# Ordering the key blocks of windowed attention by parity, in a macaron transformer kernel on one core

## What is computed

```python
w = WINDOW                                   # 32 tokens; 16 heads of 64 columns
bq, bk, bv = (t.reshape(b, h, nw, w, d) for t in (q, k, v))

def look(t):                                 # each window also sees the one before it
    p = jnp.pad(t, ((0, 0), (0, 0), (1, 0), (0, 0), (0, 0)))
    return jnp.concatenate([p[:, :, :nw], p[:, :, 1:]], axis=3)
bk2, bv2 = (look(bk), look(bv))              # 64 keys for 32 queries
mask = (it < jb) | (it > jb + w) | (jb == -1)
sim = jnp.einsum('bhwie,bhwje->bhwij', bq, bk2) * QK_SCALE
attn = jax.nn.softmax(jnp.where(mask, -jnp.finfo(sim.dtype).max, sim), -1)
out = jnp.einsum('bhwij,bhwje->bhwie', attn, bv2)
```

## Time and profile before

| | |
|---|---|
| Three runs, median | 3705.6 us |
| Lowest and highest | 3697.82 and 3710.14 us |
| Span of the profiled execution | 3698.0 us |
| Mean granted TensorE clock in it | 0.963 |
| TensorE matmul (PE) busy | 3345.2 us, 90% |
| TensorE weight load (PEld) busy | 2152.2 us, 58% |
| VectorE busy | 2824.4 us, 76% |
| GpSimd busy | 2338.6 us, 63% |
| ScalarE busy | 2242.4 us, 61% |
| DMA queue 1, share of 16 engines | 29.4%, 280.54 MB |

### The profile page before, as it was taken

The page is one execution under the profiler, slowest core; times in us unless marked ns, Lnnn a source line. Parts: engine busy times, 40 slices in busy tenths (PEclk is TensorE's granted clock), DMA queues, the critical chain, the costliest instruction groups (busy, mean ns, idle before and its releaser), DMA issues. The chain is left out here.

```text
span 3698.0 us, 147404 instructions
## 1 busy us (share of the span) xinstructions
PE 3345.2 (90%) x61692; PEld 2152.2 (58%) x61692; DVE 2824.4 (76%) x4178; ACT 2242.4 (61%) x4098; POOL 2338.6 (63%) x2167
## 2 busy tenths in 40 slices
PE   5899999999989999986998889999999999999997
PEld 2666666666666666663222566666666666666664
DVE  4888888888887888873232877878888888888883
ACT  3566766666665666652664555656666666566663
POOL 4777777776676787761000767667677767667762
PEclk8999999999999999997999999999999999999998
DMA  4334334333333333321000223333333323323321
GB/s 121 80 79 126 85 88 115 80 101 100 80 97 96 84 104 81 85 62 33 1 1 6 74 72 82 82 78 94 82 80 95 91 67 103 74 68 102 82 65 38
DMA packets 216860, 289.97 MB, mean 78 GB/s; under 512 B 61068, under 2 KB 105864, under 8 KB 215304
## 3 DMA queue, kind: packets, MB, share of 16 engines
q1 hardware_dynamic: 216200, 280.54, 29.4%
HBM read 43.43 MB, written 10.49 MB: 15 GB/s over the span
## 5 line engine op out<-in xcount | busy, mean ns | idle before, releaser
L1165 POOL TENSOR_TENSOR rot<-t 128x512 f32<-128x512 f32 x768 | 974.4, 1272 | 310.8 <-DVE t L1024 303.4
L1171 POOL TENSOR_TENSOR qkn<-rot,rn 128x512 f32<-128x512 f32 x768 | 792.1, 1042 | 180.8 <-DVE rn L1047 180.8
L1023 DVE TENSOR_TENSOR t<-ps,table 128x512 f32<-128x512 f32 x768 | 525.8, 685 | 155.2 <-ACT sq L853 148.7
L1177 POOL TENSOR_TENSOR prob<-prob,rsum 128x512 f32<-128x512 f32 x192 | 296.7, 1545 | 394.4 <-DVE rsum L1066 393.7
L1024 DVE TENSOR_TENSOR t<-ps,table 128x512 f32<-128x512 f32 x768 | 521.7, 679 | 0.0
L692 PE MATMUL sv_all<-pT,arena 64*64 64x32 f32 x24576 | 418.9, 221 | 85.4 <-issue 85.4
L624 PE MATMUL ps<-w_pair,in_hi 128*128 128x512 f16 x1152 | 450.1, 391 | 34.7 <-POOL in_lo L1192 15.7
L853 ACT ACTIVATE sq<-ps 128x512 f32<-128x512 f32 x768 | 443.3, 600 | 38.6 <-PE ps L626 36.8
L859 ACT ACTIVATE arena<-ps 128x512 f32<-128x512 f32 x384 | 226.5, 590 | 393.4 <-PE ps L626 390.2
L1030 DVE TENSOR_REDUCE n<-sq 128x16 f32<-128x1024 f32 x384 | 464.0, 1208 | 0.0
L692 PEld LDWEIGHTS sv_all<-pT,arena 64*64 64x64 f32 x24576 | 391.3, 136 | 124.5 <-issue 124.4
(11 more groups left out here) (125 smaller groups left out, 5100.3 us busy)
## 6 DMA issues: line engine op xcount, KB each, us to landing
arena<-arena SPq DMA_DIRECT2D x1152, 128.0 KB, 2.4
arena<-arena SPq DMA_DIRECT2D x768, 64.0 KB, 2.0
w_pair<-w_split SPq DMA_DIRECT2D x44, 256.0 KB, 4.6
w_stage<-in_L_ffn_Wqkv SPq DMA_DIRECT2D x6, 1536.0 KB, 8.5
w_split<-split SPq DMA_DIRECT2D x30, 256.0 KB, 2.5
wo_sb<-in_L_ffn_Wo SPq DMA_DIRECT2D x12, 512.0 KB, 4.3
xsh<-xs SPq DMA_DIRECT2D x48, 128.0 KB, 2.5
f_in<-xs SPq DMA_DIRECT2D x48, 128.0 KB, 2.2
```

The costliest lines, as they stand in the source:

```text
L1023: dve.tensor_tensor(t1[:, b, :].rearrange("p (h d) -> p h d", d=DH), src, cos, ALU.mult)
L1165: pool.tensor_tensor(rot[:, c, :], t1[:, c % 2, :], t2[:, c % 2, :], ALU.add).then_inc(pool_add, 1)
L1171: pool.tensor_tensor(qkn[:, 0, c, :].rearrange("p (h d) -> p h d", d=DH), rot[:, c, :].rearrange("p (h d) -> p h d", d=DH), rn[:, c, :].un ...
```

## The change

The 32-token blocks of the keys are ordered by parity: even blocks stand on partitions 0 to 31 and 64 to 95, odd ones on 32 to 63 and 96 to 127. For windows 1 and 3 the 64 keys are then two blocks of one 64-token group in their order; for windows 0 and 2 they are the two blocks in turned order, so `scores` reads the keys of even windows with the two blocks swapped (a view with a negative step), and the mask is swapped to match.

`values` makes one group g of 64 tokens at a time instead of one half of the heads. Its output for the lower heads goes to partitions 0 to 63 and that for the upper heads to partitions 64 to 127 of the same PSUM tile. So each of the three passes is two matmuls of 128 rows by 64 columns that stream 512 columns, where it was one of 128 by 128. `store_v` writes the group whole into `vt`. Windows 1 and 3 read `vt` directly; SyncE copies rows into `veven` for windows 0 and 2 alone, in four DMAs a tile: two of 32 partitions by 1024 elements each for even and odd blocks, of which the odd ones have 512 elements in tile s = 0, where no block comes before.

```diff
-V_DMAS = 2 * (WPT + 1)
+V_DMAS = 4
...
-                    for par in range(2):
-                        r = par * KEYS
-                        sp.dma_start(vw[r:r + WIN, p, 0, :], vtok[P - WIN:P, (s - 1) % TILES, par, :]).then_inc(v_loaded[s], 16)
-                        sp.dma_start(vw[r + WIN:r + KEYS, p, 0, :], vtok[0:WIN, s, par, :]).then_inc(v_loaded[s], 16)
-                        for w in range(1, WPT):
-                            sp.dma_start(vw[r:r + KEYS, p, w, :],
-                                         vtok[WIN * (w - 1):WIN * (w + 1), s, par, :]).then_inc(v_loaded[s], 16)
+                    for half_of in range(2):
+                        even = slice(half_of * KEYS, half_of * KEYS + WIN)
+                        odd = slice(half_of * KEYS + WIN, half_of * KEYS + KEYS)
+                        sp.dma_start(veven[even, p, :, :], vt[even, 2 * s:2 * s + 2, :]).then_inc(v_loaded[s], 16)
+                        if s:
+                            sp.dma_start(veven[odd, p, :, :], vt[odd, 2 * s - 1:2 * s + 1, :]).then_inc(v_loaded[s], 16)
+                        else:
+                            sp.dma_start(veven[odd, p, 1, :], vt[odd, 0, :]).then_inc(v_loaded[s], 16)
...
-                def values(T, q, s, half_of):
-
-                    pe.wait_ge(dve_rot, tile_done(T, 2 + half_of, 4))
-                    three_pass(proj[half_of][:, :], q, slice(s * P, (s + 1) * P),
-                               lambda w: w[:, 2 * INNER:].rearrange("p (j a r) -> p j a r", a=2, r=P)[:, :, half_of, :]).then_inc(pe_v, 1)
+                def values(T, q, s, g):
+
+                    pe.wait_ge(dve_rot, tile_done(T, 2 + g, 4))
+                    cols = slice(s * P + g * KEYS, s * P + (g + 1) * KEYS)
+                    for i, (x, w) in enumerate(((in_hi, w_hi), (in_hi, w_lo), (in_lo, w_hi))):
+                        for half_of in range(2):
+                            last = pe.matmul(proj[g][half_of * KEYS:(half_of + 1) * KEYS, :], x[:, q, cols],
+                                             w[:, 2 * INNER:].rearrange("p (j a r) -> p j a r", a=2, r=P)[:, :, half_of, :],
+                                             start=i == 0, stop=i == 2, skip_group_check=True)
+                    last.then_inc(pe_v, 1)
...
+                                keys = kT[r, p, pair, w * WIN:w * WIN + KEYS]
+                                if w % 2 == 0:
+                                    keys = keys.rearrange("d (b k) -> d b k", b=2)[:, ::-1, :]
...
+                                keys = vt[r, 2 * s + w // 2, :] if w % 2 else veven[r, v, w // 2, :]
...
-                    act.activation(vtok[:, s, par, :], proj[par][:, :], ACT.Copy, scale=1.0 / W_SCALE).then_inc(act_v, 1)
+                    act.activation(vt[:, 2 * s + g, :], proj[g][:, :], ACT.Copy, scale=1.0 / W_SCALE).then_inc(act_v, 1)
...
-    first[:WIN, :WIN] = MASKED
+    first[:WIN, WIN:] = MASKED
```

More of the change, by code:

```diff
@@ L133, in build @@
         kT = sb("kT", [P, 2, PAIRS, WIN + P])
-        arena = sb("arena", [P, 4 * WPT * CH])
-        vw = arena[:, 0:2 * WPT * CH].rearrange("p (a w c) -> p a w c", a=2, w=WPT)
-        vtok = arena[:, 2 * WPT * CH:].rearrange("p (s a c) -> p s a c", s=TILES, a=2)
+        arena = sb("arena", [P, 7 * P * 8])
+        vt = arena[:, 0:2 * TILES * CH].rearrange("p (s c) -> p s c", s=2 * TILES)
+        veven = arena[:, 2 * TILES * CH:(2 * TILES + 4) * CH].rearrange("p (a w c) -> p a w c", a=2, w=2)
         smax = sb("smax", [P, HEADS])
@@ L664, in scores @@
                                 r = slice(par * DH, (par + 1) * DH)
+                                keys = kT[r, p, pair, w * WIN:w * WIN + KEYS]
+                                if w % 2 == 0:
+                                    keys = keys.rearrange("d (b k) -> d b k", b=2)[:, ::-1, :]
                                 last = pe.matmul(sv[par][w * WIN:(w + 1) * WIN, pair * KEYS:(pair + 1) * KEYS],
-                                                 qT[r, p, pair, w * WIN:(w + 1) * WIN],
-                                                 kT[r, p, pair, w * WIN:w * WIN + KEYS],
+                                                 qT[r, p, pair, w * WIN:(w + 1) * WIN], keys,
                                                  start=False, stop=True, skip_group_check=True)
@@ L691, in outputs @@
                                 r = slice(half_of * KEYS, (half_of + 1) * KEYS)
+                                keys = vt[r, 2 * s + w // 2, :] if w % 2 else veven[r, v, w // 2, :]
                                 last = pe.matmul(sv[half_of][par * DH:(par + 1) * DH, j * P + w * WIN:j * P + (w + 1) * WIN],
-                                                 vw[r, v, w, j * P + par * DH:j * P + (par + 1) * DH],
+                                                 keys[:, j * P + par * DH:j * P + (par + 1) * DH],
                                                  pT[r, 4 * par + j, w * WIN:(w + 1) * WIN],
@@ L853, in squares, with store_v @@
                     act.activation(sq[:, c, :], proj[c % 2][:, :], ACT.Square).then_inc(act_sq, 1)
-                def store_v(T, B, s, par):
+                def store_v(T, B, s, g):
                     act.wait_ge(pe_pv, tile_done(T - TILES))
                     act.wait_ge(v_loaded[(s + 1) % TILES], windows_done(B if s == 3 else B - 1))
-                    act.wait_ge(pe_v, tile_done(T, par, 2))
-                    act.activation(vtok[:, s, par, :], proj[par][:, :], ACT.Copy, scale=1.0 / W_SCALE).then_inc(act_v, 1)
+                    act.wait_ge(pe_v, tile_done(T, g, 2))
+                    act.activation(vt[:, 2 * s + g, :], proj[g][:, :], ACT.Copy, scale=1.0 / W_SCALE).then_inc(act_v, 1)
                 def log_norm(T):
@@ L1260, in layer @@
                     body(STEADY, B + 3, None if last else 0, L_next, L_split, 4)
-                pool.memset(vtok[P - WIN:P, TILES - 1, :, :], 0.0).then_inc(v_zeroed, 1)
+                pool.memset(veven[:, 0, 0, :], 0.0).then_inc(v_zeroed, 1)
                 pool.wait_ge(v_zeroed, half + 1)
@@ L1561, in window_masks @@
     m = np.where((i < j) | (i > j + WIN), MASKED, 0.0)
-    inner = np.tile(m, (WPT, 1))
+    turned = np.concatenate([m[:, WIN:], m[:, :WIN]], 1)
+    inner = np.concatenate([m if w % 2 else turned for w in range(WPT)])
     first = inner.copy()
-    first[:WIN, :WIN] = MASKED
+    first[:WIN, WIN:] = MASKED
     return np.ascontiguousarray(np.stack([inner, first], 1).astype(np.float32))
```

## The result

| | before | changed |
|---|---|---|
| Median of four runs each, us | 3701.71 | 3755.41 |
| Lowest and highest, us | 3693.5, 3710.14 | 3748.54, 3758.87 |
| Span of the profiled execution, us | 3698.0 | 3757.1 |

The account below looks back on a forecast made before the run. TensorE was taken as the bound, its queue almost without pause. 3698.0 + 79 (layout) + 3 (code) gave 3780 us; from the runs' median 3787, less 7 for replaced waits, again 3780 us, range 3740 to 3830 us.

Parts of the forecast that it names:

- The bound: Whole kernel: TensorE, busy 90% of 3698.0 us, sets the end; work added to its queue moves the end.
- the rival with 3715 us: TensorE's queue: its waits for VectorE and GpSimd absorb most of the 79 us of layout costs; 7% chance.
- Side by side: In values: the two 64-column matmuls of a pass run concurrently, so nothing is streamed longer.
- the bound of 327 us: In values: upper bound if each half matmul ran alone, six more of 0.215 us a tile.
- the two rivals with 4033 and 4015 us: In values: halves run one after the other (4033 us, 7%); or loads are exposed, 12 a tile (4015 us, 3%).
- the layout: TensorE around values: changing to, within and from column tiles costs 0.41 us a tile, 78.7 us in all.
- Entering and leaving: Around a values group: passing into a tiled layout costs 0.09 us, out of it 0.10 us.
- The copies at nothing: SyncE's value copies: four DMAs a tile for ten, 94 MB for 201 MB, costed at nothing.
- Code: TensorE's instruction fetch: 2304 more instructions lengthen the stops for code by 3 us, scatter 14 us either way.
- Waits that shrink: TensorE's 78.5 us of waits for other engines: the longer queue replaces a tenth, 7 us.
- The sum: Whole kernel: 3698.0 + 79 + 3 = 3780 us on the profiled execution.
- Faster, by fewer stops: TensorE's stops for code: less queue 1 traffic brings code sooner; 30 stops instead of 119 give 3665 us; 5% chance.

Follow-up runs that it names:

- e2: The kernel before with only the copies changed: four DMAs a tile of the change's sizes in place of ten; 0.993, 21 us under it at the medians.
- the one-group kernel: The changed kernel with group 0 of values as before, three matmuls of 128 by 128, and only group 1 in column tiles; 1.0144 to the kernel before.

## Why the prediction was right, point by point

**The bound.** TensorE sets the end, and what is added to its queue shows. Right: the column tiles alone cost 73 us. So they do not hide behind other engines, and the rival with 3715 us is out.

**Side by side.** Right: the two halves of a pair start together, pairs start 0.24 and 0.21 us apart (medians), and the bound of 327 us is excluded. The loads lie under the stream in the same row group; the two rivals with 4033 and 4015 us are out. The trace speaks here against what the Trainium skill says ("TensorE: Matmul & The Clock Gate", part 3, the mechanism), which was named with the second: tiles of one row group take their loads while they stream, and the third pair in the step above starts 0.46 us after the first, its loads at 2549.47 us, before the second pair has streamed.

**The term that was mis-sized** is the layout: 0.41 us a tile, measured 0.34, 65 us for 79. Entering and leaving were exact, 0.09 and 0.10. Wrong was "0.025 us by the two decimals, twice in a group of three passes, 0.05 us": the two passes lose 0.03 together, and the last part, 0.01 for the second matmul of the pair, is not to be seen in the hundredths. The group up to its follower, "some 0.9 us", is 0.86 us.

**The copies at nothing.** Wrong in size: e2 gains 0.7%, from a cause that stays open. The cover that I named, SyncE's idle time, was there and proves nothing about traffic. This and the smaller layout term are why 54 us came and not 75: 14 us less for the layout, 21 to 26 us for the copies, and up to 13 us the other way for the clock. That errors of both signs met is luck; the mechanism, a dearer layout on the engine that sets the end, is not.

**Code.** I put 3 us on it, with 14 us either way. The stops grew by 3.7 us. That was luck in part: the scatter is real, as the shifted code (15 us) and the one-group kernel (19 us of such waits) show. I had not priced the low clock behind the stops, up to 13 us here.

**Waits that shrink.** I took 7 us; the rows fell by 8.9, from 78.5 to 69.6.

**The sum** for the profiled execution is 3698.0 + 65 + 4 + 13 - 9 = 3771; it was 3757.1. The 14 us left over have the sign of the copies, and the 13 us of clock are an upper bound; the profile doesn't divide them.

**Faster, by fewer stops** did not come: 121 of them, where fewer than 58 would have been needed. That fewer copies would bring code sooner is refuted by e2.

## What to carry to other kernels

On an engine whose queue never pauses, count changes of tile layout as work: each cost 0.09 to 0.10 us here, also between two tiled layouts, so products of one layout should stand together and full-width ones outside. A DMA that nobody waits for can still cost some tenths of a per cent; make it alone before you cost it at nothing. And before trading a stop inside a burst for a later end of that burst, look who waits for its end.

## What was not expected of the hardware

- 96 waits that are long fulfilled, placed before the work, made the kernel slower by 0.4% (1.0026 to 1.0053), though they cost no time where they stand (74.3 us against 74.2 to the first product of `scores`); they shift the code against its packets, and the stops for code lie 256 instructions, or a multiple, apart.
- Fewer and smaller copies within the chip's memory gave 0.7%, with stops unchanged (161.4 us against 160.3) and a clock that explains at most 10 of the 21 to 26 us; half the bytes alone gave 0.2%, fewer DMAs of the same bytes nothing that shows.
- Leaving a tiled layout for another one took 0.31 us to the next start, the same as leaving it for the full width.
